# A two-layer graph network with its dense node ranges chosen per layer: four built and kept in layer one, a fifth built in layer two

## The reference

```python
def _sage_conv(x, src, dst, W_l, b_l, W_r):
    msgs = x[src]
    agg = jax.ops.segment_sum(msgs, dst, num_segments=N_NODES)
    deg = jax.ops.segment_sum(jnp.ones((src.shape[0],), x.dtype), dst, num_segments=N_NODES)
    mean = agg / jnp.maximum(deg, 1.0)[:, None]
    return mean @ W_l + b_l + x @ W_r
h = jax.nn.relu(_sage_conv(x, src, dst, W1_l, b1, W1_r))
h = jax.nn.relu(_sage_conv(h, src, dst, W2_l, b2, W2_r))
return h @ W3 + b3          # and outside: x = layernorm(x + this)
```

## Time and profile before

| | us |
|---|---|
| median of 3 runs | 4425.2 |
| lowest, highest | 4417.39, 4447.91 |
| the profiled execution, its own time | 4420.95 |
| its span, first to last instruction | 4419.1 |
| mean granted TensorE clock, share of full | 0.857 |

### The profile page before, as it was taken

One profiled execution on the slowest core, in us unless ns is written; L12 is line 12 of the kernel. 1 busy time (PEld: TensorE's weight loads), 2 busy tenths in 40 slices (PEclk: granted clock), 3 DMA queues, 4 the chain that ended last, 5 costly groups with the idle time before them and its releaser, 6 DMA issues. The chain is left out here.

```text
span 4419.1 us, 64045 instructions
## 1 busy us (share of the span) xinstructions
PE 3179.9 (72%) x12648; PEld 2286.4 (52%) x12649; DVE 1682.1 (38%) x4452; ACT 482.2 (11%) x1411; POOL 2392.4 (54%) x2456
## 2 busy tenths in 40 slices
PE   4777877787777777877777666766767667766766
PEld 1453645464545454655555455555545455555544
DVE  8637363636362535343322222222222222222222
ACT  2000000000000000100001011111111111111111
POOL 2443545454544455455564655666656566666654
PEclk7888998899888898988998778888888788888888
DMA  2251525252525253444454544445444454544445
GB/s 73 65 161 55 177 79 175 76 169 77 170 71 167 80 175 109 146 133 129 142 173 131 157 140 153 150 147 160 149 153 144 133 154 144 156 149 146 150 141 153
DMA packets 341994, 597.79 MB, mean 135 GB/s; under 512 B 48212, under 2 KB 253002, under 8 KB 340499
## 3 DMA queue, kind: packets, MB, share of 16 engines
q0 software_dynamic: 117504, 321.02, 24.5%
q1 hardware_dynamic: 172274, 223.09, 15.8%
q10 hardware_dynamic: 52000, 51.21, 3.8%
HBM read 536.91 MB, written 58.22 MB: 135 GB/s over the span
## 5 line engine op out<-in xcount | busy, mean ns | idle before, releaser
L471 PE MATMUL psA<-ring,oh 128*125 128x257 f32 (+1 forms) x6416 | 1805.4, 439 | 730.1 <-DVE oh L849 485.1
L471 PEld LDWEIGHTS psA<-ring,oh 128*125 128x125 f32 x6416 | 1358.1, 218 | 1133.1 <-issue 891.4
L397 POOL DMA_INDIRECT ring<-in_x,scol x1224 | 1187.5, 970 | 1210.4 <-PE psA L471 830.7
L397 POOL DMA_INDIRECT ring<-z_rows,scol x1224 | 1204.2, 984 | 785.2 <-issue 338.6
L849 DVE SCALAR_TENSOR_TENSOR oh<-dcol,cf,iota 128x500 f32<-128x500 int16 x802 | 595.4, 742 | 1415.4 <-PE psA L471 531.4
L498 PE MATMUL psB<-oh 128*128 128x490 bf16 x1016 | 344.3, 438 | 294.7 <-DVE oh L881 230.1
L881 DVE TENSOR_SCALAR oh<-iota,cf,key 128x490 bf16<-128x490 int16 x1016 | 422.7, 416 | 14.8 <-issue 13.1
L835 DVE TENSOR_TENSOR acc<-psA,acc x806 | 337.1, 418 | 36.4 <-issue 31.7
L498 PEld LDWEIGHTS psB<-oh 128*128 128x128 bf16 x1016 | 74.1, 103 | 533.8 <-DVE oh L881 395.3
L879 DVE TENSOR_SCALAR oh<-iota,key 128x128 bf16<-128x128 int16 x1016 | 263.9, 260 | 218.5 <-issue 141.6
L526 PE MATMUL psB<-xs,cnt_a 128*125 128x257 f32 x980 | 246.0, 395 | 42.0 <-DMA xs<-in_x 35.9
(11 more groups left out here) (123 smaller groups left out, 1143.3 us busy)
## 6 DMA issues: line engine op xcount, KB each, us to landing
xs<-in_x SPq DMA_DIRECT2D x120, 512.0 KB
cnt_a<-z_rows SPq DMA_DIRECT2D x70, 768.0 KB
counts<-cnt_a SPq DMA_DIRECT2D x10, 3185.0 KB
cnt_a<-counts SPq DMA_DIRECT2D x70, 455.0 KB
work<-in_x ACTq DMA_DIRECT2D x200, 125.0 KB
ring<-in_x,scol POOLq DMA_INDIRECT x1224, 3.8
ring<-z_rows,scol POOLq DMA_INDIRECT x1224, 6.8
z_rows<-work ACTq DMA_DIRECT2D x100, 125.0 KB
```

What stands on the lines that cost most here:

```text
L397: pool.indirect_dma_start(ring[:, slot, b, 0:D], None, rows_dram, bass.IndirectOffsetOnAxis(scol[:, n - C0:n - C0 + 1], 0)).then_inc(rows_ ...
L471: mm = pe.matmul(psA[0:WN, bass.ds(bank, W)], oh[:, 2 * (slot % 2) + later, b, :], ring[:, slot, b, 0:W], start=(b == 0), stop=(b == nb - 1))
```

## The change

Each layer gets its own `HW`, `HB` and set of groups. Layer one treats windows 0 to 3 densely and gathers from block 300 on: 8 halves, 316 groups. A half now has 36 groups woven in, 24 in its build (a chunk after every second group) and 12 with an `x_step`. 28 groups follow. Window 4 is summed sparsely in layer one.

Layer two keeps windows 0 to 4 and 306 groups. It first builds window 4's two halves itself, with 28 groups each as layer one had, and multiplies them with the rows of `z_dram`. Then it streams the four kept matrices in 28 iterations of 4 groups, a `z_step` after every second group. 138 groups follow, 28 of them with the fallback steps. In SP's program the function `place` takes the role of `free`. The set-up makes a table of groups for each layer. The last gather's own semaphore (`rows_end`) goes.

```diff
-HW = 5
-HB = 340
+HW = (4, 5)
+HB = (300, 340)
+G0 = tuple(b // GB for b in HB)
+NGL = tuple(NG - g for g in G0)
...
+BUILD = (6, 4)
+HALF = tuple(4 * n + STEPS for n in BUILD)
+HALVES = (2 * HW[0], 2 * (HW[1] - HW[0]))
+BUILT = ((1, 3), (0, 1, 2))
+YITER = HW[0] * FC // 2
+BACK = (NGL[0] - HALVES[0] * HALF[0], NGL[1] - HALVES[1] * HALF[1] - 4 * YITER)
...
+            users = [0]
+            last_use = {}
+
+            def place(*buffers, reads=()):
+
+                need = max(last_use.get(k, 0) for k in buffers)
+                if need:
+                    sp.wait_ge(s_xused, need)
+                users[0] += 1
+                for k in buffers + reads:
+                    last_use[k] = users[0]
+
+            def half_matrix(l, rows_dram, part):
+
+                for t in range(STEPS):
+                    j, nj = xs_step(t)
+                    j += part % 2 * JH
+                    at = xs_at(t)
+                    if l == 0 and t == 2:
+                        sp.wait_ge(s_bank, credit[s_bank] + part * (CH + 1) + CH)
+                        sp.dma_start(a_dram[part], scratch).then_inc(s_kept, 16)
+                    place("xs%d" % (t % 2), reads=("counts",))
...
+            for part in range(HALVES[1]):
+                half_matrix(1, z_dram, part)
+            sp.wait_ge(s_kept, 16 * HALVES[0])
+            for i in range(YITER):
+                for q in range(2):
+                    n = 2 * i + q
+                    j = n % FC * FJ
+                    place("lin%d" % q, "counts")
+                    sp.dma_start(lin_a[:, q].rearrange("p j n -> p (j n)"),
...
                     for q in range(2):
                         pool.wait_ge(s_zd[q], 16 * (NW // 2))
-                for g in range(NGG):
+                for g in range(NGL[l]):
...
+                with pe.Fori(0, HALVES[l]):
+                    chunk(CJ)
+                    with pe.Fori(0, BUILD[l]):
+                        for i in range(4):
                             one_group(i)
-                            x_step(i)
+                            if i in BUILT[l]:
+                                chunk(CJ)
                             if i % 2:
                                 finish(until)
-                else:
-                    with pe.Fori(0, HW * FC // 2):
-                        for i in range(8):
+                    for i in range(STEPS):
+                        one_group(i)
+                        x_step(l, i)
+                        if i % 2:
+                            finish(until)
+                if l == 1:
+                    with pe.Fori(0, YITER):
+                        for i in range(4):
                             one_group(i)
-                            if i % 4 == 3:
-                                z_step(i // 4)
                             if i % 2:
+                                z_step(i // 2)
                                 finish(until)
-                with pe.Fori(0, FC // 2 - 1):
+                with pe.Fori(0, FC // 2):
                     for i in range(4):
                         one_group(i)
                         if i % 2:
                             fallback(l)
                             finish(until)
-                for i in range(NGG - REST % 4, NGG):
+                if BACK[l] >= 2 * FC + 4:
+                    with pe.Fori(0, BACK[l] // 4 - FC // 2):
+                        for i in range(4):
+                            one_group(i)
+                            if i % 2:
+                                finish(until)
+                for i in range(BACK[l] % 4):
                     one_group(i)
-                    if i >= NGG - 2:
-                        fallback(l)
```

More of the change, by code:

```diff
@@ L363, in _, with fallback @@
+            def fallback(rows_dram, c):
+                place("xs0", "xs1")
+                blocks(xs[:, 0:FJ - 1, 0:D], rows_dram, c * FJ, FJ - 1, s_fall)
+                last_block(xs[:, FJ - 1, 0:D], rows_dram, c * FJ + FJ - 1, s_fall)
+            sp.wait_ge(s_set, 1)
+            for part in range(HALVES[0]):
+                half_matrix(0, x, part)
+            for c in range(FC):
+                fallback(x, c)
             for q in range(2):
                 sp.wait_ge(s_zd[q], 16 * (NW // 2))
-            n1 += FC
@@ L376, in _ @@
+            for c in range(FC):
+                fallback(z_dram, c)
         @block.gpsimd
@@ L399, in _ @@
                             bass.IndirectOffsetOnAxis(scol[:, n - C0:n - C0 + 1], 0)).then_inc(
-                                rows_end[l] if g == NGG - 1 and b == GB - 1 else rows[l][slot], 16)
+                                rows[l][slot], 16)
         @block.tensor
@@ L460, in _, with pair @@
                 pe.reg_mov(r, 0)
-            def pair(l, slot, nb, later, end):
+            def pair(l, slot, nb, later):
                 W = RW if l == 0 else D
@@ L513, in chunk, with x_step @@
                 with pe.If(1 < pe.snap(more)):
[L514 removed]
+                    with pe.Fori(1, pe.snap(more, min_val=1, max_val=HB[1])):
                         count_blocks(n, False)
[L517 removed]
+            def x_step(l, t):
+                W = RW if l == 0 else D
                 j, nj = xs_step(t)
@@ L1021, in layer @@
-                        v.reg_alu(at_w, part, 1, ALU.logical_shift_right)
-                        add_hot(l, v.snap(at_w, min_val=0, max_val=HW - 1))
-                else:
-                    with v.Fori(0, HW * FC // 2) as part:
-                        for i in range(8):
+                    keep_counts(JH)
+                    for i in range(STEPS):
+                        group(l, i, GB)
+                        if i % 2:
+                            finish(until)
+                    if l == 0:
+                        v.reg_add(kept, kept, 16)
+                        v.wait_ge(s_kept, v.snap(kept, min_val=16, max_val=16 * HALVES[0]))
@@ L1026, in layer @@
+                    v.reg_add(xdone, xdone, STEPS)
+                    v.wait_ge(s_xused, v.snap(xdone, min_val=1, max_val=1 << 24))
+                    v.reg_alu(at_w, part, 1, ALU.logical_shift_right)
+                    if l == 1:
+                        v.reg_add(at_w, at_w, HW[0])
+                    add_hot(l, v.snap(at_w, min_val=0, max_val=HW[1] - 1))
+                if l == 1:
+                    with v.Fori(0, YITER) as part:
+                        for i in range(4):
                             group(l, i, GB)
```

388 lines of the change are left out of this document (174 added, 214 removed).

## The result

The changed kernel takes 4699.1 us (median of 4 runs, 4677.1 to 4709.7), the kernel before 4427.7 us (4 runs, 4417.4 to 4447.9): ratio 1.060, 95% interval 1.055 to 1.066. It is slower by 272 us; I had forecast 4325 us, 100 us faster.

What follows compares the result with a forecast made beforehand. No engine is full: a chain of hand-overs bounds the kernel, with GpSimd's gathers a floor of 5.05 us a group. Layer one -98 us and layer two 0 take the profiled 4421 to 4323, median 4325 us; range 4260 to 4380.

Steps and rivals of the forecast that it cites:

- 2, 3: Layer one: 64 groups placed in eight builds at 4.5 us each, 288 us, plus 4 us of set-up.
- rival C: Layer two's streaming: each load comes to stand in series, up to 7 us a step, 4632 us in all; chance 0.13.
- three signs of being wrong: Layer one ends at 2380 us; the 28 add_hot lie 33 us or more apart; free run stays at 6 us.
- Step 1: Layer one drops window 4's two halves, with 56 groups and their chunks: -402 us.
- Step 2: Layer one places 66 groups again: 64 in builds at 4.5 us, 288 us (262 to 384), two behind, 12 us.
- Step 4: Layer two builds window 4 itself: 56 groups at 402 us instead of 360, +42 us (+20 to +70).
- Step 5: Layer two streams windows 0 to 3 with 112 groups at 7.2 us, loads covered: +85 us (0 to +155).
- Step 6: Layer two's last 138 groups, 110 with gathers alone at 5.3 us each: -127 us (-154 to -50).
- H: Theory formed after the result: TensorE's releases come late while gathers are being issued; a pause lets them through.
- the 1.4 us over the floor: Layer two's streaming: loss per group, 6.43 us against GpSimd's gather floor of 5.05, laid to the iteration.

Runs made afterwards that it cites:

- Nine: The changed kernel as it is, rerun on a third chip beside the kernel before: 3977.8 us, ratio 1.040.
- Thirteen: The kernel before, unchanged, profiled on a fourth chip: 3813.4 us, one run.
- One: The changed kernel with two streamed loads in flight again in layer two, on a chip like the first: 4620.1 us, ratio to the kernel before 1.042.
- Ten: The changed kernel with two streamed loads in flight again, on the third chip: 3903.2 us, ratio to the kernel before 1.022.
- Six: The kernel before with only layer two's packing changed, a streamed half after each 2 groups instead of 4, second chip: 3811.5 us, ratio 0.998.
- (3): The kernel before with one ordinary 128 KB DMA issued by GpSimd after each group's four gathers, chip like the first: 4266.9 us, ratio 0.963.
- (2): The fills: the kernel before with four GpSimd fills of a spare tile after each group's four gathers, chip like the first: 4248.2 us, ratio 0.958.
- Eleven: The kernel before with four GpSimd fills of an unused tile after each group's gathers, on the third chip: 4255.1 us, ratio 1.111.

## Why the prediction was wrong

Both pairs of traces, made from the same marks, against my terms (us, after less before, rounded so that the columns add up; the times are those of `add_hot`, of the last gather of layer one and the first and last of layer two, and the span's end):

| step | forecast | first chip | others (Nine less Thirteen) |
|---|---|---|---|
| 1: window 4's halves leave layer one | -402 | -402 | -338 |
| 2, 3: 64 groups put beside the builds, and set-up | +292 | +488 | +317 |
| 2: two groups behind | +12 | +20 | +29 |
| layer one | **-98** | **+106** | **+8** |
| 4: window 4 built in layer two | +42 | +17 | +17 |
| 5: streaming, 112 groups | +85 | +127 | +142 |
| 6: the last 138 groups | -127 | +20 | -11 |
| layer two | **0** | **+164** | **+148** |
| between the layers and at the end | 0 | +12 | +11 |
| whole | **-98** | **+282** | **+167** |

How the first chip's column comes about: the eighth `add_hot` falls at 1839.9 us before and at 2328.2 after, +488, and from the last one to the last gather of layer one pass 156 us before and 176 after. Layer two's stretches are those shown with the result. The last column has 1984.5 less 1667.1 = 317; Thirteen's tenth `add_hot` at 2005.3, 338 after its eighth; last gathers of layer one at 2141.0 and 2133.2, so 157 less 128; and the stretches shown above. Nine and Thirteen ran on two chips; on Nine's own chip the change costs 158 us (medians).

The measured 4699 us lies above my range and above rival C's 4632 too. Of my three signs of being wrong two came, layer one ending late (2504 us, I had said 2380) and a free run at over 6 us a group. The third didn't: the 28 `add_hot` lie 30.4 us apart, under the 33 us that I had named.

*Step 1* is a reading of the trace of before and no forecast; on Thirteen's chip the same two halves take 338 us.

*Step 2 failed, and on the first chip it failed most*: "I take 4.5 us" a group, from VectorE's distance in a light build, within 4.1 to 6.0. Measured, with the set-up in it, are 317/64 = 5.0 us on the chips where releases come at once and 488/64 = 7.6 us on the first, above my upper bound of 6.0, which was layer one's tail. So 64 groups cost nearly what two halves had taken on the other chips (338 us), and more than they had taken on the first (402). 4.1 us was one distance in a queue that runs in bursts: in the same build the distances after the earlier trace rows go on with 9.7 us (2086.82 to 2096.55). The whole build, 126 us for 16 groups, is 7.9 us a group with its chunks, and as an upper bound it would have held. That the 2.6 us between the two kinds of chip are held releases is argued from the kernel before: there the fills bring layer one's end from 2398 to 2228 us on the first chip, as on the third with the same fills (2235). In the changed kernel it wasn't tested on the first chip.

*Step 4 held in its mechanism*; the 104 marks among layer two's gathers cost 17 us where I gave 42. The Trainium skill's "SBUF — State Buffer", section "SBUF: two separate sides", would have had them in GpSimd's way, if they are two-port instructions, which no run shows. The trace again shows nothing of it: in the stretch of after with these marks a gather takes 229.01/236 = 0.970 us, without them, in the streaming, 433.06/448 = 0.967.

*Step 5 failed in a statement and in its size.* "It is covered as long as TensorE's two groups in between take longer than the load": TensorE waited 94 us for loads (49 in Nine), and undoing the wait gave 79 us on the first chip, 75 on the third. Groups come in bursts: with the wait undone, 10 of the 55 intervals between two streamed products are under 5.5 us in One and 15 of 55 in Ten, the shortest 3.3 us, while a load takes some 7 us. That is what rival C names; my argument against it, that the ring can't stay full at 10.1 us for two gathered groups, holds for the mean alone. C's mechanism was there, at a fifth of its price. The rest of this row, 142 less 75 = 67 us on the other chips, lies in streaming at 5.9 us a group in Ten (28 iterations in 660.4 us), where Thirteen has 5.3. TensorE is at 77% of that stretch in Nine, 82% in Ten, and GpSimd waits for it. Six packs as closely and needs only 5.4 us (34 iterations from 2211.5 to 2939.6 us), with 0.2 us a group less of TensorE's records (Ten, then Six):

```profile
2487.00:3147.00 660.00, 538.63 (x2248) 441.53 (x2248) 191.69 (x394) 100.32 (x331) 433.23 (x448) 0.92 0.70 220
...
2177.00:2940.00 763.00, 642.66 (x2782) 532.27 (x2782) 237.32 (x485) 116.10 (x379) 554.91 (x569) 0.94 0.75 239
```

Why Ten is the slower of the two I can't say.

*Step 6 failed outright.* I gave the free groups 5.3 us instead of 6.2 and won 127 us. On the other chips they do cost 712/138 = 5.2 us, but groups with a streamed half cost 5.2 to 5.3 there as well (723/138 in the same place of Thirteen): GpSimd sets the pace with or without the load, so freeing groups of it buys nothing, as Six shows by itself (0.998). On the first chip they cost 6.4 us, where the same groups with loads had cost 860/138 = 6.2. So what made them dearer than the floor was not the load; by H it was the held releases, which a free run has as well. I had charged the 1.4 us over the floor to the iteration and its transfers; the rows with "remote" named another cause.

*Is H shown?* That on the first chip releases of TensorE stand behind gathers is what the counts over the traces, the 1.18 us of each added gather and the gain by the fills agree on, and that the fills gain nothing where no release is late ties the pause's effect to the releases. (3) gains almost as much with most releases still late, so H doesn't explain every gain. Two rivals are in the traces. The clock (0.857 against 0.921) comes with longer records of TensorE, 3180 us in all against 2984 in Thirteen, which is 196 of the 608 us between the spans at the most. Gathers land later (median 5.3 us after issue against 4.5), but TensorE waits less for them, 115 us against 244. That the first chip's slower layer one comes from it, in the kernel before, (2) and Eleven show between them; for layer two, where the fills take as much as they free, and for the changed kernel's 488 less 317 us it is argued from the same signs. The change's own loss doesn't need H: 167 us of 282 are there without it, nearly all in layer two. Why one chip does this and three don't stays open, and so does whether it is the chip or something that ran beside it. Whether the fills would help the changed kernel on the first chip wasn't measured. No version tried beats the kernel before on both kinds of chip: the fills win 4% on one and lose 11% on the other; the packing alone is level where it was measured.

## What to carry to other kernels

Before a stage is freed of work, ask whether the engine that sets its pace (here GpSimd, 5.05 us of gathers a group) ever waited for that work; if not, the work was riding for nothing, and packing it more closely elsewhere buys nothing (Six, 0.998) and can cost (Ten, 1.022). Bound the price of an item added among others by the mean of a whole stage that holds such items, not by one distance within a burst, and check a claim "covered" against the shortest interval, not the mean. And read a releaser that the profile can't name as a term of its own: here it was the longest wait of ScalarE's copy (910 us) and pointed at the late releases.

## What the runs showed of the hardware

The same program took 4430 us on one chip and 3815 on three others, at equal durations of its gathers (0.984 and 0.983 us) and with a clock of 0.857 against 0.921. On the slower one, ScalarE's copy, which waits for TensorE alone, started up to 11.4 us after the record of the transposes when they ended in a run of gathers (40 of 51 late in the changed kernel), and mostly 0.04 us after it otherwise (33 of 34); on the others at most 0.16 us, gathers or not (Nine and Thirteen, 147 copies). A pause of 1.3 us after four gathers gave 4% back there, and made the kernel as fast or slow as on the other kind of chip: 4248 and 4255 us. One ordinary DMA of 128 KB after four gathers gave back 3.7% there; elsewhere it wasn't tried.
